# Router logits of eight tiles in f32r from the split transposed rows, and four tiles fewer to transpose in the second FFN

## Reference

```
x = x + 0.5 * ffn(layernorm(x))
x = x + mixer(layernorm(x))
x = x + 0.5 * ffn(layernorm(x))

def ffn(x):
    shared = silu(x @ Ws_gate) * (x @ Ws_up) @ Ws_down           # 704 wide
    scores = softmax(x @ W_router)                               # 512 x 8
    topk_vals, topk_idx = top_k(scores, 2)
    combine = einsum(topk_vals, one_hot(topk_idx))
    routed = sum over 8 experts of combine * ((silu(x @ We_gate) * (x @ We_up)) @ We_down)   # 352 wide
    return routed + shared
```

## Time and profile before

| | us |
|---|---|
| median of 3 runs | 1646.93 (1641.62 to 1650.94) |
| the profiled execution | 1653.21 |
| its span, first to last instruction | 1651.4 |
| TensorE busy in it | 1558.2 |
| VectorE, ScalarE, GpSimd busy | 1036.1, 751.5, 795.0 |
| mean granted TensorE clock | 0.972 |

### The profile page before, as it was taken

One profiled execution on the slowest core, in us unless ns is written; L12 is line 12 of the kernel. 1 busy time (PEld: TensorE's weight loads), 2 busy tenths in 40 slices (PEclk: granted clock), 3 DMA queues, 4 the chain that ended last, 5 costly groups with the idle time before them and its releaser, 6 DMA issues. The chain is left out here.

```text
span 1651.4 us, 24820 instructions
## 1 busy us (share of the span) xinstructions
PE 1558.2 (94%) x9018; PEld 1328.3 (80%) x9018; DVE 1036.1 (63%) x1712; ACT 751.5 (46%) x1290; POOL 795.0 (48%) x475
## 2 busy tenths in 40 slices
PE   6989999999999989989888999999989999999999
PEld 6767999999877777787767778778768999999877
DVE  6564565666476956667556766765664666666465
ACT  4211666666424544545255345434212666666411
POOL 2111777766444346435423553452111777766442
PEclk9999999999999999999899999997989999999999
DMA  7032677777352110120011002014032677777243
GB/s 285 26 105 65 240 265 269 252 267 269 107 186 83 64 53 1 39 77 1 1 53 65 1 20 71 2 36 147 26 105 79 235 256 277 250 273 275 89 153 128
DMA packets 70876, 214.49 MB, mean 130 GB/s; under 512 B 8096, under 2 KB 8096, under 8 KB 69856
## 3 DMA queue, kind: packets, MB, share of 16 engines
q1 hardware_dynamic: 48672, 155.18, 26.4%
q0 software_dynamic: 11360, 37.23, 7.6%
q10 hardware_dynamic: 10720, 20.45, 3.4%
HBM read 179.80 MB, written 33.03 MB: 129 GB/s over the span
## 5 line engine op out<-in xcount | busy, mean ns | idle before, releaser
L618 POOL TENSOR_TENSOR g_lo<-g_raw,g_hi 128x1408 fp32r<-128x1408 f32 x54 | 180.0, 3333 | 262.5 <-ACT g_hi L745 262.2
L618 POOL TENSOR_TENSOR u_lo<-u_raw,u_hi 128x1408 fp32r<-128x1408 f32 x54 | 174.1, 3224 | 68.6 <-ACT u_hi L745 68.6
L1642 PE MATMUL bank<-u_hi,xgT 128*128 128x352 f32 x624 | 169.5, 333 | 0.0
L1642 PE MATMUL bank<-g_hi,xgT 128*128 128x352 f32 x624 | 162.8, 323 | 0.0
L1665 PE MATMUL bank<-d_hi,hT 128*128 128x512 f32 (+1 forms) x468 | 160.2, 396 | 1.5 <-DVE hT L1046 1.4
L683 POOL TENSOR_TENSOR w_hl<-w_raw,w_hl 128x1024 fp32r<-128x1024 f32 x36 | 88.1, 2446 | 150.6 <-ACT w_hl L745 150.6
L1594 PE MATMUL bank<-xs,g_hi 128*128 128x512 f32 (+1 forms) x384 | 128.7, 418 | 7.1 <-DVE gate L1192 6.2
L1610 PE MATMUL bank<-d_hi,hT 128*128 128x512 f32 (+1 forms) x384 | 125.6, 400 | 4.9 <-DVE hT L1046 2.5
L793 ACT ACTIVATE gate<-bank 128x512 f32<-128x512 f32 (+1 forms) x48 | 28.6, 595 | 222.4 <-PE bank L1594 213.3
L1377 DVE SCALAR_TENSOR_TENSOR acc<-pre,cw,acc 128x512 f32<-128x512 f32 x120 | 121.7, 1014 | 4.3
L1046 DVE TENSOR_TENSOR hT<-bank,hT 128x384 fp32r<-128x384 f32 x78 | 43.1, 552 | 129.2 <-ACT hT L745 129.2
(11 more groups left out here) (246 smaller groups left out, 3722.5 us busy)
## 6 DMA issues: line engine op xcount, KB each, us to landing
g_raw<-in_w_gate SPq DMA_DIRECT2D x54, 704.0 KB, 5.6
u_raw<-in_w_up SPq DMA_DIRECT2D x54, 704.0 KB, 6.3
d_raw<-in_w_down SPq DMA_DIRECT2D x54, 512.0 KB, 4.9
w_raw<-in_w_in SPq DMA_DIRECT2D x37, 512.0 KB, 3.2
routed_y<-ys ACTq DMA_DIRECT2D x32, 512.0 KB, 4.8
d_raw<-in_w_down SPq DMA_DIRECT2D x54, 192.0 KB, 5.5
token_x<-xn SPq DMA_DIRECT2D x8, 1024.0 KB, 5.1
X<-in_x SPq DMA_DIRECT2D x4, 1024.0 KB, 9.7
```

Source lines behind the costliest of these rows:

```text
L618: pool.tensor_tensor(half_of(piece, 1, s), raw_at[piece][s % RING][:], half_of(piece, 0, s).bitcast(F), ALU.subtract)\
L1642: ins = pe.matmul(dst[:, 0:FE], xgT[:, n % 2, hx, kc], half_of(piece, hw, NS + j)[:, kc], start=(m == 0), stop=(m == 3 * KD - 1))
```

## The change

The logits of tiles 0 to 7 are made from the halves in xs, in f32r: for each chunk the high rows are multiplied with both halves of the router weights side by side (wr_hl, 16 columns), and the low rows with the high half (8 columns). Bank 4 has 16 columns for each tile now, and shift_logits adds the second eight to the first for those tiles. Tiles 8 to 15 keep tmpT and float32. The logits of tiles 0 to 3 move from the head into slot 0 of job 0, those of 4 to 7 into slot 1, and slots 2 to 5 have two tiles each as before (ROUTED_AT). In the second FFN tiles 0 to 3 are not transposed. r_hl_u moves to the place of r_cmp.

```
+    wr_hl = sb("wr_hl", [P, KD, 2 * NE], R)
+    ROUTED_AT = [range(0, TB), range(TB, 2 * TB)] + [range(t, t + 2) for t in range(2 * TB, NT, 2)]
 (GpSimd, ahead of the row gathers)
-                pool.wait_ge(n_tp, (nf + 1) * NT)
+                pool.wait_ge(n_tp, (nf + 1) * NT - nm * TB)
 (ScalarE)
+            act.activation(wr_hl[:, :, 0:NE], wr[:], ACT.Copy).then_inc(n_whi, 1)
                 def x_copy(t):
-                    n = nf * NT + t
-                    act.wait_ge(n_tp, n + 1)
-                    if t >= 2:
-                        act.wait_ge(n_lg, n - 1)
-                    act.activation(tmpT[t % 2][:], bank[5 + t % 3][:], ACT.Copy).then_inc(n_cp, 1)
-                    if nm * TB <= t < 2 * TB:
+                    act.wait_ge(n_tp, nf * NT - nm * TB + t + 1)
+                    if t < 2 * TB:
                         split_hi(xs[t // TB][:, 0, :, t % TB * P:(t % TB + 1) * P],
                                  bank[5 + t % 3][:].rearrange("p (c t) -> p c t", c=KD), b_hi)
+                    else:
+                        if t >= 2 * TB + 2:
+                            act.wait_ge(n_lg, nf * NT + t - 1)
+                        act.activation(tmpT[t % 2][:], bank[5 + t % 3][:], ACT.Copy).then_inc(n_cp, 1)
-                for t in range(TB):
+                for t in range(nm * TB, TB):
                     x_copy(t)
 (VectorE)
                 def shift_logits():
-                    logits = bank[4][:, 0:NT * NE].rearrange("p (t e) -> p t e", e=NE)
+                    logits = bank[4][:, 0:2 * NT * NE].rearrange("p (t e) -> p t e", e=2 * NE)
                     dve.wait_ge(n_lg, (nf + 1) * NT)
-                    own.step(dve.tensor_reduce(r_1[:], logits, AX.X, ALU.max))
-                    dve.tensor_tensor(r_a[:], logits, each(r_1[:], NE), ALU.subtract).then_inc(n_sh, 1)
+                    own.mark(dve.tensor_copy(r_a[:], logits[:, :, 0:NE]))
+                    own.join()
+                    own.step(dve.tensor_tensor(r_a[:, 0:2 * TB], r_a[:, 0:2 * TB], logits[:, 0:2 * TB, NE:], ALU.add))
+                    own.step(dve.tensor_reduce(r_1[:], r_a[:], AX.X, ALU.max))
+                    dve.tensor_tensor(r_a[:], r_a[:], each(r_1[:], NE), ALU.subtract).then_inc(n_sh, 1)
                 block_scale(0)
+                if k == 0:
+                    dve.wait_ge(n_whi, 1)
+                    lo_half(wr_hl[:, :, NE:], wr[:], wr_hl[:, :, 0:NE], n_wlo)
                 block_stats(1)
 (TensorE)
                 def logits(t):
-                    pe.wait_ge(n_cp, nf * NT + t + 1)
+                    at, both = t * 2 * NE, slice(t % TB * P, (t % TB + 1) * P)
+                    if t >= 2 * TB:
+                        pe.wait_ge(n_cp, nf * 2 * TB + t - 2 * TB + 1)
+                    elif t >= nm * TB:
+                        pe.wait_ge(b_lo0, nf * 2 * TB - nm * TB + t + 1)
                     for c in range(KD):
-                        ins = pe.matmul(bank[4][:, t * NE:(t + 1) * NE], tmpT[t % 2][:, c * P:(c + 1) * P], wr[:, c],
-                                        start=(c == 0), stop=(c == KD - 1))
+                        if t >= 2 * TB:
+                            ins = pe.matmul(bank[4][:, at:at + NE], tmpT[t % 2][:, c * P:(c + 1) * P], wr[:, c],
+                                            start=(c == 0), stop=(c == KD - 1))
+                        else:
+                            pe.matmul(bank[4][:, at:at + 2 * NE], xs[t // TB][:, 0, c, both], wr_hl[:, c],
+                                      start=(c == 0), stop=False)
+                            ins = pe.matmul(bank[4][:, at:at + NE], xs[t // TB][:, 1, c, both], wr_hl[:, c, 0:NE],
+                                            start=False, stop=(c == KD - 1))
                     ins.then_inc(n_lg, 1)
                 def transpose_x(tiles):
                     for t in tiles:
                         pe.wait_ge(n_xn, nf * NT + t + 1)
-                        if t >= 3:
-                            pe.wait_ge(n_cp, nf * NT + t - 2)
-                            pe.wait_ge(b_lo0, nf * 2 * TB - nm * TB + min(t - 2, 2 * TB))
+                        if t - 3 >= 2 * TB:
+                            pe.wait_ge(n_cp, nf * 2 * TB + t - 2 - 2 * TB)
+                        elif t - 3 >= nm * TB:
+                            pe.wait_ge(b_lo0, nf * 2 * TB - nm * TB + t - 2)
                         transpose(5 + t % 3, xn[:, t], n_tp)
                 def router(half):
-                    for t in PAIRS[half]:
+                    if half == 0:
+                        pe.wait_ge(n_wlo, 1)
+                    for t in ROUTED_AT[half]:
                         logits(t)
-                transpose_x(range(2))
-                for t in range(TB):
-                    logits(t)
-                    if t + 2 < TB:
-                        transpose_x(range(t + 2, t + 3))
+                transpose_x(range(nm * TB, TB))
                 transpose_x(PAIRS[0])
```

More of the change, by code:

```diff
@@ L134, in program @@
     row_of = sb("row_of", [P, SLOTS], U32)
-    r_hl_u = sb("r_hl_u", [P, 2, TOPK * NT], U32)
     r_hl = sb("r_hl", [P, 2, TOPK * NT])
@@ L223, in program @@
     r_in = nc.alloc_sbuf_tensor_at("r_in", [P, SLOTS, NE], F, offset=r_idx[:].tensor.manual_sbuf_range[0])
+    r_hl_u = nc.alloc_sbuf_tensor_at("r_hl_u", [P, 2, TOPK * NT], U32, offset=r_cmp[:].tensor.manual_sbuf_range[0])
     r_out = nc.alloc_sbuf_tensor_at("r_out", [P, SLOTS, NE], F, offset=r_a[:].tensor.manual_sbuf_range[0])
@@ L316, in program @@
     n_lg = sem("n_lg")
+    n_whi = sem("n_whi")
+    n_wlo = sem("n_wlo")
     n_sh = sem("n_sh")
@@ L1698, in free @@
                             pe.wait_ge(n_sh, nf + 1)
-                            pe.wait_ge(n_cp, (nf + 1) * NT)
+                            pe.wait_ge(n_cp, (nf + 1) * 2 * TB)
                         if job:
```

## The result

The changed kernel takes 1657.51 us, median of ten runs (1649.71 to 1662.27), beside 1649.89 for the kernel before in ten runs of its own (1641.62 to 1653.98). The ratio is 1.0055, with a 95% interval of 1.0035 to 1.0075: between 5.8 and 12.4 us slower. The forecast was +9.6.

What follows compares the result with a forecast made beforehand. TensorE, busy 94% of the span, was taken as the bound. Work of +3.2 us in the first FFN and +3.0 in the second, +6.2, plus +3.4 of clock made +9.6: 1656.5 us against the median, range 1648 to 1664.

Steps and rivals of the forecast that it cites:

- (a): Slots 0 and 1 of job 0: four tiles of logits each instead of two, 0.114 us a pair; +3.64 us per FFN.
- R3: Rival: f32r weights load as fast as bf16, so not slower; about -3 us, 1644 us, chance 0.12.
- (b): Job 0 waits covered: tile 4's low half, -0.6 us in the first FFN; tmpT at the fifth slot, -0.5 in each.
- (c): First FFN's head: fewer ScalarE copies, one VectorE row delays u_lo, added router-weight work; +0.1 us, between -1.5 and +0.5.
- (d): Second FFN's head: transposes of tiles 4 and 5 start 1.5 us earlier, at half clock; -0.75 us.
- (e): Softmax's front: shift_logits' added copy and add delay the chain and the down matmuls; +0.6 us in each FFN.
- (g): Granted clock: three falls at the four slots of four tiles against one costly before, net two; +3.4 us.
- R1: Rival: the clock does not mind, only the +6.2 us of work remain; 1653.1 us, chance 0.20.
- R2: Rival: the clock stays low over whole slots, four at about 3 us; +16.5 us, 1663.4 us, chance 0.15.
- R4: Rival: second FFN's first logits wait, the halves are not what is read; +0.75 us on any case, no own chance.

Runs made afterwards that it cites:

- head_logits: Changed kernel with logits of tiles 0 to 3 (first FFN: 0 to 2) moved from slot 0 into the heads; 1654.94 us, ratio 1.0028 to the kernel before.
- full: Changed kernel with logits in the heads, first gate half ahead of the second block's transposes, other tiles in slots of up to three; 1658.54 us, ratio 1.0044.
- best: Changed kernel with logits in the heads, third block's statistics before the second block's rows, and high rows against 256 columns; 1647.37 us, ratio 0.9987.
- best2: Order of full plus the third block's early statistics, 256-column high rows and tile 4's transposes in slot 0; 1648.64 us, ratio 0.9997.
- best3: best with the early statistics in the second FFN only; 1648.91 us, ratio 0.9996 to the kernel before.
- keep_transposes: Changed kernel with tiles 0 to 3 transposed again in the second FFN, read by nobody; 1658.66 us, ratio 1.0044 to the kernel before.
- the second measurement: The changed kernel unaltered, timed again beside the kernel before; median 1658.41 us, ratio 1.0042.
- wide_high: Changed kernel with the high rows' matmul of tiles 0 to 7 widened from 16 to 256 columns; 1653.36 us, ratio 1.0020 to the kernel before.
- double_pairs: Changed kernel with each matmul pair of tiles 0 to 7 issued twice; 1685.67 us, ratio 1.0194 to the kernel before.

## Why the prediction was right, step by step

**(a), +3.64 us in each FFN: right.** The pairs start 0.1115 us apart at full clock, 3.48 us for slot 1 with its 32; I took 0.114. The f32r loads for these matmuls last 192 ns in the median, as the fp32 ones do. R3, cheap f32r loads, is out. The rule that spoke for it, in the Trainium skill, "TensorE: Matmul & The Clock Gate", section "Weight-path perf modes" (fast load for any type but FP32), is not what these rows show for f32r: 192 ns for 128 columns, where bf16 has 95.

**(b), -0.6 and -0.5: right where counted.** The waits are gone in the changed kernel, and come back at 0.77, 0.48, 0.65 and 0.50 us when half of the pairs go.

**(c), +0.1: -0.3 measured** (24.75 beside 25.04; 24.48 in the second trace). Inside its bounds. The row that gets in between moves the end of u_lo by 0.19 us, not by the 0.5 that I took. TensorE runs the first gate matmuls at half speed until about 29.5 us in this execution and until 27.3 in that of before, so the gate half takes 5.05 us (24.75 to 29.80) instead of 3.90 (25.04 to 28.94), which is 1.2 of the +5.0 us of the first FFN. Executions with the same head switched anywhere between 26.5 and 29.8 us, so I take that for chance and not for the change.

**(d), -0.75: the start right, what it is worth open.** The start moved by 1.45 us, as forecast, and I halved it because the clock was low there. In the traces the head gave more: the clock rose 14.3 us behind the residual, not 17.7 as in the one trace of before, and the gate half took 3.74 us instead of 4.62, together 2.3 us. But the rise came 14.3 us behind the residual in nine traces of the changed kernel and its variants, head_logits with logits in the head among them, and sooner in the other four (full, best, best2, best3). Either the later rise of before belongs to its order of work, and the head gave 2.3, or it is that execution's alone, and 0.75 stands. One trace of before can't tell. The transposes, which I took for part of the gain, are none of it: keep_transposes has them and starts as early.

**(e), +0.6: right.** Copy and add put the reduction 0.58 us later, and TensorE's wait ahead of down is 0.6 us longer.

**(g), three falls against one, +3.4 us: right in place and number, the price mis-sized.** Falls came at three of the four slots, in both traces of the changed kernel. Over the executions of the second measurement the time at 0.50 grew by 11.2 us, just over three falls of 3.41, at 0.39 for each us: 4.4 us. wide_high gives 3.6 by the ratios, uncertain by 4. The forecast counted two net falls, at 0.5 us for each us. It left out the falls while down runs, which both traces of the changed kernel have in both FFNs. Too few falls and too high a price partly cancelled, and that is luck.

**The sum.** Forecast 6.2 of work and 3.4 of clock; by the second measurement 3.7 and 4.4. Of the 2.5 us less of work, 0.4 is (c), and up to 1.6 may be (d) with the clock's rise. The rest I can't place; it is less than the second measurement leaves uncertain, 2.8 us on either side. So the total of +9.6 agrees with +7.6 and +8.1 within the noise, while the work came out smaller and the clock's share larger than forecast. R1, the clock doesn't mind, is refuted by the falls in the slots themselves and by double_pairs (27.3 us where its pairs make 14.3); the total alone would not refute it, since R1's +6.2 lies in the interval of 5.8 to 12.4. R2 happens with the pairs doubled, and in the first FFN of the trace of keep_transposes, so it is part of what an execution of the changed kernel's slots can do, but not the rule in the three traces with these slots; R4, the second FFN's halves are not what is read, doesn't show: there is no wait at its slot 0.

On the rival rule for the clock: the Trainium skill, "TensorE: Matmul & The Clock Gate", table of "Why this matters for your kernels", ties drops to gaps in which TensorE is idle. The fall at 32.94 us here came with TensorE busy without a gap from 24.75 us on, and the same pairs with a wider matmul brought none. Idle gaps are not the only cause in this kernel.

## What to carry to other kernels

A matmul with few columns costs what its weight load takes (0.11 us a pair for 128 columns, in f32r as in fp32), so f32r in place of fp32, or fewer moving columns, buy nothing; ask what the edit does to the number of loads, and where they stand. Logits are free in a head where TensorE waits for VectorE and cost their full length in a full stretch, less the waits that they cover there; moving them from the one to the other is where the change's added work comes from. A dense block of such small matmuls can bring the clock down by itself: measure the time at 0.50 over many executions before one trace's places are believed, and, where a load can have more columns behind it, try that: here it took the falls out of the slots.

## What the chip showed that I had not expected

- The granted clock falls behind a stretch of narrow matmuls in which TensorE is never idle: 32 pairs with 16 and 8 columns, 0.1115 us apart, brought falls to 1.2 GHz in three of four slots, in both traces of the changed kernel and in that of keep_transposes; the same 32 loads with 256 columns in half of the matmuls, 0.114 us apart, brought none in those of wide_high, best and best3 (best2 has falls behind slots of three tiles, which hold fp32 logits too). In time, wide_high is 3.6 us faster by the ratios, uncertain by 4.
- A microsecond at 1.2 GHz costs 0.39 us of time in the kernel before on average, not the 0.5 of an engine that is always the bound (29 executions, correlation 0.97; the changed kernel's 22 give 0.31). The spread of its time, 1642.77 to 1658.24 us, nearly all goes with this.
- At the start TensorE works at half speed up to 26.5 to 29.8 us from execution to execution, while the granted clock stands at 1.00 in those rows, in the traces of before and after. The row can't tell that there; in the traces of head_logits, full and best3, with logits in the first head, it does show 0.50.
- A VectorE operation that is pending when GpSimd goes from one long operation to the next gets in between; one that comes later waits until the next has ended: the gate starts at 26.93 and 27.23 us in the kernels with early statistics, at 24.4 to 24.8 in the changed kernel and the variants without (full and best2, with the gate ahead of those transposes, aside).
